# A two-part f16 GRU on one core: the candidate's matmul with both parts side by side, split into two matmuls onto one set of columns

## The reference

```python
def step(h, xs):
    xzt, xrt, xht = xs
    z = jax.nn.sigmoid(xzt + h @ U_z + vz)
    r = jax.nn.sigmoid(xrt + h @ U_r + vr)
    hh = jnp.tanh(xht + r * h @ U + vh)
    h_new = (1.0 - z) * h + z * hh
    return (h_new, h_new)
```

## Time and profile before

| | us |
|---|---|
| median of 2 runs | 6571.26 |
| the runs | 6569.87 and 6572.66 |
| the profiled execution | 6569.49 |
| its span, first to last instruction | 6567.7 |
| PE matmul / weight load busy | 5848.3 / 5500.4 |
| DVE / ACT busy | 5242.4 / 3454.6 |
| mean granted clock of PE | 0.997 |

### The profile page before, as it was taken

One profiled execution on the slowest core, in us unless ns is written; L12 is line 12 of the kernel. 1 busy time (PEld: TensorE's weight loads), 2 busy tenths in 40 slices (PEclk: granted clock), 3 DMA queues, 4 the chain that ended last, 5 costly groups with the idle time before them and its releaser, 6 DMA issues.

```text
span 6567.7 us, 486051 instructions
## 1 busy us (share of the span) xinstructions
PE 5848.3 (89%) x200312; PEld 5500.4 (84%) x200312; DVE 5242.4 (80%) x39096; ACT 3454.6 (53%) x23405; POOL 7.8 (0%) x22
## 2 busy tenths in 40 slices
PE   7888888888888888888888888888888888888888
PEld 7888888888888888888888888888888888888888
DVE  6888888878888888887888887888878888788887
ACT  3555555555555555555555555555555555555555
POOL 0000000000000000000000000000000000000000
PEclk8999999999999999999999999999999999999999
DMA  2000000000000000000000000000000000000000
GB/s 84 19 19 16 19 18 19 18 19 16 19 18 19 18 18 18 19 19 18 17 18 19 18 19 16 19 18 19 19 18 16 19 19 18 18 18 19 18 19 18
DMA packets 80316, 129.98 MB, mean 20 GB/s; under 512 B 12336, under 2 KB 18480, under 8 KB 80304
## 3 DMA queue, kind: packets, MB, share of 16 engines
q1 hardware_dynamic: 80304, 129.81, 5.7%
HBM read 20.46 MB, written 8.65 MB: 4 GB/s over the span
## 4 chain that ended last, share of the span: by engine, by line
DVE 50%; PE 31%; ACT 10%; issue 8%; DVEq 1%; POOL 0%; POOLq 0%
PE pair_r L299 31%; DVE rh_part L571 11%; DVE h_part L571 7%; DVE rh_part L578 7%; DVE pair_r L562 6%; DVE h_part L601 5%; DVE ps_z L562 5%; DVE pair_h L566 4%; ACT r_scan L434 4%; DVE h_part L609 3%; ACT pair_r L389 3%; ACT th_z L406 2%; DVEq L647 1%; PE ps_z L255 0%; DVE y_next L529 0%
## 5 line engine op out<-in xcount | busy, mean ns | idle before, releaser
L299 PEld LDWEIGHTS pair_r<-h_part,u_part 128*128 128x128 f16 x65568 | 1779.5, 96 | 1038.7 <-DVE h_part L571 1033.8
L299 PE MATMUL pair_r<-h_part,u_part 128*128 128x48 f16 (+1 forms) x65568 | 1976.9, 183 | 693.2 <-DVE h_part L571 686.5
L299 PE MATMUL pair_h<-rh_part,u_part 128*128 128x48 f16 (+1 forms) x65536 | 1953.4, 183 | 0.0
L299 PE MATMUL ps_z<-h_part,u_part 128*128 128x48 f16 (+1 forms) x65568 | 1942.9, 183 | 1.3 <-issue 1.3
L299 PEld LDWEIGHTS pair_h<-rh_part,u_part 128*128 128x128 f16 x65536 | 1797.6, 96 | 0.0
L299 PEld LDWEIGHTS ps_z<-h_part,u_part 128*128 128x128 f16 x65568 | 1784.7, 96 | 1.4 <-issue 1.4
L406 ACT ACTIVATE r_scan<-pair_r 128x4 f32<-128x4 f32 x4098 | 720.6, 176 | 1955.2 <-DVE pair_r L562 1752.6
L566 DVE TENSOR_REDUCE pair_h<-pair_h 128x4 f32<-128x8 f32 x4096 | 714.4, 175 | 549.9 <-PE pair_h L299 549.9
L562 DVE TENSOR_REDUCE pair_r<-pair_r 128x4 f32<-128x20 f32 x4098 | 766.5, 187 | 428.6 <-PE pair_r L299 2.7
L571 DVE TENSOR_TENSOR_SCAN rh_part<-r_scan,rh_part 128x12 f16<-128x12 f32 x4098 | 749.6, 183 | 140.5
L406 ACT ACTIVATE th_z<-ps_z 128x8 f32<-128x8 f32 x2048 | 362.7, 177 | 893.7 <-DVE ps_z L562 893.7
(11 more groups left out here) (75 smaller groups left out, 3111.3 us busy)
## 6 DMA issues: line engine op xcount, KB each, us to landing
w_stage<-w_in SPq DMA_DIRECT2D x384, 256.0 KB, 2.3
x_tok<-in_x SPq DMA_DIRECT2D x68, 128.0 KB, 2.6
out_dram<-o_tok SPq DMA_DIRECT2D x66, 128.0 KB, 2.3
mlp_w<-in_L_cond_W SPq DMA_DIRECT2D x2, 1024.0 KB, 6.8
u_raw<-in_L_cond_U_r SPq DMA_DIRECT2D x1, 1024.0 KB, 5.8
u_raw<-in_L_cond_U_z SPq DMA_DIRECT2D x1, 1024.0 KB, 7.8
u_raw<-in_L_cond_U SPq DMA_DIRECT2D x1, 1024.0 KB, 10.2
w_in<-in_L_cond_W_r SPq DMA_DIRECT2D x4, 256.0 KB, 9.6
```

Of the source, the lines that this page charges most:

```text
L299: return nc.tensor.matmul(to[:, :, :, 0:run], u_part[:, g, part, k, gm * P:(gm + 1) * P], runs.unsqueeze(1).broadcast_to([P, repeats, n, r ...
```

## The change

Each tile of H becomes two matmuls with the same weights, first the high parts, then the low parts, both onto the same PSUM columns, where they add up by themselves; each has 24 columns (the 12 of one part, streamed twice). With the sum already in the product's columns, DVE's two `candidate_total` and their semaphores go, and ACT's tanh reads the columns of the product directly, two by two at a stride, after PE's own signal. The zero slot of `xp` goes too, and with it the copy of zeros in H's seed. Because the tanh now reads the columns that H's next seed writes, ACT waits for the end of its second tanh before that seed.

```diff
-        xp = sb("xp", [P, GM, 2 * TB, 2, B])
+        xp = sb("xp", [P, GM, 2 * TB, B])
...
-            runs = banks.rearrange("p (m c) -> p m c", c=H_SLOT)[:, :, WIDE - PARTS * RUN:WIDE]
-            return runs.rearrange("p m (a c) -> p m a c", c=RUN)[:, :, :, STEP - 1:STEP * B:STEP]
+            return banks.rearrange("p (m c) -> p m c", c=H_SLOT)[:, :, STEP - 1:STEP * B:STEP]
...
-            nc.gpsimd.memset(xp[:, :, :, :, :], 0.0).then_inc(s["h0_ready"], 1)
+            nc.gpsimd.memset(xp[:, :, TB:2 * TB, :], 0.0).then_inc(s["h0_ready"], 1)
...
-                n = ADDENDS[g] if g == H else ADDENDS[g] - 1
+                n = PARTS if g == H else ADDENDS[g] - 1
                 at = k // HC * n * PITCH + k % HC * B * STEP
-
+                weights = u_part[:, g, part, k, gm * P:(gm + 1) * P]
+                runs = parts[:, at:at + n * PITCH].rearrange("p (a c) -> p a c", c=PITCH)
+
+                if g == H:
+
+                    repeats, run = (1, B * STEP) if closing else (WIDE // (n * RUN), RUN)
+                    to = bank[:, H_SLOT * m:H_SLOT * m + repeats * RUN].rearrange("p (r c) -> p r c", c=RUN)[:, :, 0:run]
+                    for a in range(n):
+                        last = nc.tensor.matmul(to, weights, runs[:, a, 0:run].unsqueeze(1).broadcast_to([P, repeats, run]),
+                                                start=False, stop=False, skip_group_check=True)
+                    return last
...
             def tanh(to, bank, g, n, wait, t1, done):
                 act.wait_ge(s[wait], t1)
-                at = H_SUM if g == H else SUM
-                A(to, bank[:, at:at + n], ACT.Tanh, scale=scale_reg[g]).then_inc(s[done], 1)
+                if g == H:
+                    A(to.rearrange("p (m b) -> p m b", b=B), candidate_cols(bank), ACT.Tanh, scale=scale_reg[g]).then_inc(s[done], 1)
+                else:
+                    A(to, bank[:, SUM:SUM + n], ACT.Tanh, scale=scale_reg[g]).then_inc(s[done], 1)
...
-                    tanh(n_scan[:, half[0], 1], ps_h[0], H, HS, "h0_sum", t1, "h0_th")
+                    tanh(n_scan[:, half[0], 1], ps_h[0], H, HS, "h0_mm", t1, "h0_th")
                     seed(ps_z, Z, nxt)
-                    tanh(n_scan[:, half[1], 1], ps_h[1], H, HS, "h1_sum", t1, "h1_th")
+                    tanh(n_scan[:, half[1], 1], ps_h[1], H, HS, "h1_mm", t1, "h1_th")
                     if proj is not None and u == K:
                         act.wait_ge(s["xp_ok"], act.snap(proj[2] + 1))
+
+                    act.wait_ge(s["h1_th"], t1)
                     seed(pair_h, H, nxt)
...
-            def candidate_total(hf):
-                V.tensor_reduce(ps_h[hf][:, H_SUM:H_SUM + HS].rearrange("p (m b) -> p m b", b=B),
-                                candidate_cols(ps_h[hf]).rearrange("p m a b -> p m b a"), AX_X, ALU.add).then_inc(s[f"h{hf}_sum"], 1)
...
-                dve.wait_ge(s["h0_mm"], t1)
-                candidate_total(0)
-
                 dve.wait_ge(s["z_keep"], t1)
...
-                dve.wait_ge(s["h1_mm"], t1)
-                candidate_total(1)
```

More of the change, by code:

```diff
@@ L110, in gru_kernel @@
         SUM = 256
-        H_SLOT, H_SUM = 256, 128
+        H_SLOT = 256
         def cols(bank, g, m0, m1):
@@ L127, in gru_kernel @@
                  "x_in x_tr y_ok y_copied proj0_mm proj0_ok wst_in proj_mm xp_ok o_sum o_tr o_ev out_st "
-                 "seed0 h_open h0_ready r0_mm r1_mm z_mm z_keep h_ok h0_mm h1_mm r0_sum r1_sum z_sum h0_sum h1_sum r0_th r1_th z_th h0_th h1_th "
+                 "seed0 h_open h0_ready r0_mm r1_mm z_mm z_keep h_ok h0_mm h1_mm r0_sum r1_sum z_sum r0_th r1_th z_th h0_th h1_th "
                  "rhi0 rhi1 rh0 rh1 khi keep_ok nhi0 nhi1 hs0 hs1 copied scan_zero rh_zero")
@@ L290, in tile @@
             def tile(bank, m, g, gm, k, part, parts, first=False, closing=False):
-                n = ADDENDS[g] if g == H else ADDENDS[g] - 1
+                n = PARTS if g == H else ADDENDS[g] - 1
                 at = k // HC * n * PITCH + k % HC * B * STEP
+                weights = u_part[:, g, part, k, gm * P:(gm + 1) * P]
[7 more added lines that the diff above has]
+                    return last
                 repeats, run = (1, B * STEP) if closing else (WIDE // (n * RUN), RUN)
-                runs = parts[:, at:at + n * PITCH].rearrange("p (a c) -> p a c", c=PITCH)[:, :, 0:run]
-                end = (H_SLOT if g == H else SLOT) * m + WIDE
+                end = SLOT * m + WIDE
                 to = bank[:, end - repeats * n * RUN:end].rearrange("p (r a c) -> p r a c", a=n, c=RUN)
-                return nc.tensor.matmul(to[:, :, :, 0:run], u_part[:, g, part, k, gm * P:(gm + 1) * P],
-                                        runs.unsqueeze(1).broadcast_to([P, repeats, n, run]),
-                                        start=first and g != H, stop=False, skip_group_check=True)
+                return nc.tensor.matmul(to[:, :, :, 0:run], weights,
+                                        runs[:, :, 0:run].unsqueeze(1).broadcast_to([P, repeats, n, run]),
+                                        start=first, stop=False, skip_group_check=True)
             def staggered(banks, g, parts, src, name, t1):
@@ L380, in seed @@
             def seed(banks, g, at):
+                src = xp[:, g * K:(g + 1) * K, at, :]
                 if g == H:
-                    return A(candidate_cols(banks.rearrange("p h c -> p (h c)")),
-                             xp[:, g * K:(g + 1) * K, at].rearrange("p m a b -> p m a b"), ACT.Copy)
-                src = xp[:, g * K:(g + 1) * K, at, 0]
+                    return A(candidate_cols(banks.rearrange("p h c -> p (h c)")), src, ACT.Copy)
                 if g == Z:
@@ L404, in tanh @@
                 act.wait_ge(s[wait], t1)
-                at = H_SUM if g == H else SUM
-                A(to, bank[:, at:at + n], ACT.Tanh, scale=scale_reg[g]).then_inc(s[done], 1)
+                if g == H:
+                    A(to.rearrange("p (m b) -> p m b", b=B), candidate_cols(bank), ACT.Tanh, scale=scale_reg[g]).then_inc(s[done], 1)
+                else:
+                    A(to, bank[:, SUM:SUM + n], ACT.Tanh, scale=scale_reg[g]).then_inc(s[done], 1)
             def store_projection(i, ring, bb):
-                return A(xp[:, i, bass.ds(ring, TB), 0, bb], ps_p[:, bb * TB:(bb + 1) * TB], ACT.Identity,
+                return A(xp[:, i, bass.ds(ring, TB), bb], ps_p[:, bb * TB:(bb + 1) * TB], ACT.Identity,
                          bias=v_bias[:, i, bb:bb + 1])
@@ L553, in _ @@
                 for bb in range(B):
-                    V.tensor_tensor(xp[:, g * K:(g + 1) * K, 0:TB, 0, bb], src[:, :, :, bb],
+                    V.tensor_tensor(xp[:, g * K:(g + 1) * K, 0:TB, bb], src[:, :, :, bb],
                                     v_bias[:, g * K:(g + 1) * K, bb:bb + 1].broadcast_to([P, K, TB]),
```

## The result

The changed kernel takes 7833.39 us (7829.21 and 7837.57), the kernel before 6571.26: the ratio is 1.1919, 95% interval 1.1891 to 1.1948. The profiled execution took 7829.21 us for a span of 7826.9. The forecast was 7705 in 7610 to 8100.

The account below looks back on a forecast made before the run. No engine alone bounds the kernel; a serial loop hands over between engines 2048 times. Steps of 3.72 us (3.14 + 0.58) give 7618.6, plus 82.6 around them 7701, and a slow first step makes 7705 us, range 7610 to 8100.

Parts of the forecast that it names:

- The spacing: PE's H product: each pair of weight load and 24-column matmul takes 25.0 ns, bounds 10 to 27.
- Half 1's chain: H's end, ACT's tanh, DVE's high part and scan, then R's second part: +0.58 us, step 3.14 to 3.72 us.
- The pause inside R: Sign on PE: R waits inside itself for half 1, about 0.2 to 0.3 us.
- The cover: Half 0's tanh, high part and R's first 13 matmuls, and the projection, hide behind half 1: no cost.
- The z chain: Z's tanh and factors on ACT, DVE's keep product: covered, ready at 3008.35, wanted at 3008.80.
- The sums' removal: DVE loses two candidate sums of 0.17 us each per step: gain 0.02 us a step, 40 us in all.
- rival A: PE's H spacing halves with the columns or dropped second loads; only the sums' removal remains: 6530 us. Chance 0.08.
- Rival C: PE is short of instructions, supply limited to the present mean rate: 4.2 us a step, 8730 us. Chance 0.04.
- B: PE's granted clock falls, 1.2 GHz throughout giving 4.47 us a step, 9240 us, or anything between. Chance 0.08.
- half 1's high part 3.61 us behind the start of R: Sign on DVE: if the high part starts at another distance, the sum is wrong in its second term.

Follow-up runs that it names:

- looped kernel: Changed kernel with PE's three plain steps of an outer turn as one step in a loop of 3, outputs transposed behind it: 7711.97 us, ratio 1.1741.

## Why the prediction was right, and where it was off

**The spacing** was taken as 25.0 ns, since 20 ns of columns already did not set it. (The rows, 184 - 173, give 11 ns for 24 columns and not 10, so 21 to 22 for 48, still less than 25.) Measured: 25.2 ns in the changed kernel's H stage, 24.9 by the kernel with 48 H matmuls. Every pair had its own load, as the identity's rows had suggested (265848 matmuls and 265848 loads). The Trainium skill (TensorE: Matmul & The Clock Gate, Back-to-back issue gap) was read too narrowly in the prediction: the section gives its formula for a matmul by itself, says that it counts too little for pairs of load and matmul at few columns, and its table puts 1 to 64 columns at a floor of about 25 ns. So it did not speak for the change, and the trace agrees with that floor at 24 columns as at 48.

**Half 1's chain.** From H's start the forecast had 1.78 us to the tanh and 1.99 to the high part; both were met to 0.01 us. The pause inside R was to be 0.2 to 0.3 us: it is 0.22 us between the starts of the 13th and 14th matmul behind a projection, and 0.34 without one (medians). The step was forecast at 3.72 and was 3.72 (looped kernel: 7711.97 us against 7701 of the sum). Step by step this part is right, and three kernels show it from three sides: fewer projections and a later half 0 change nothing, and 16 H matmuls less take their 25 ns each off.

**The cover.** Half 0 and PE's own issue cost nothing, as forecast (the kernels with half 0 closed later and with fewer projections). The z chain was not tried by itself, but DVE's product with its factor starts at 3016.60 in the changed kernel's trace, 0.45 us ahead of half 0's first use of DVE.

**The sums' removal** was the mis-sized term of rival A: 0.02 us a step in the text, 0.048 measured. It entered nothing but the rival's time, 6530 for 6476.63.

**The sum's missing term** is code: 116 us of the 128 by which 7833.39 exceeds 7705; of the rest, 7 us are what the looped kernel takes beyond the forecast, and 5 the difference between two measurements of the changed kernel. The range held the result, but its top had been set for a wider spacing and a clock that falls, not for this. That 116 us fit into it is luck. Rival C said that PE could be short of instructions, but as a supply rate, and it was dismissed because 25 ns held over 96 pairs. That says something on the rate and nothing on whether a loop's code stays. The number that would have decided it is the size of PE's outer body, 9 x 192 instructions growing to 9 x 256. The clock's fall is a follower of that pause: without the pauses the mean was 0.997. The text had said that a granted clock below 1 in the loop proves B. It was below 1 (0.62 in a window of 8 us) and did not prove B, which had the clock fall in steps without a pause. The narrower matmuls only made the time at the lower clock longer.

**A criterion that was badly put.** The text wanted half 1's high part 3.61 us behind the start of R. It is not: in the step shown it is 3017.70 - 3013.77 = 3.93, since R's start moves with the projection. From Z it is 3017.70 - 3014.91 = 2.79 us, for 2.21 before, and that is the +0.58.

## What to carry to other kernels

At the full clock a matmul of few columns costs its place in the stream and not its columns: two of 24 columns cost 50 ns where one of 48 cost 25. (At 1.2 GHz one of 48 took 39.7.) So splitting one to save a reduction pays only if that reduction stands on the path for longer than all the added matmuls. What the reduction is worth must be asked in both kernels: here it was worth 0.05 us a step before and 0.20 us after the split. And count the instructions of the longest loop body on each engine before adding to it: on PE the step over the limit cost more than 3 us in each turn, and folding plain steps into an inner loop took it back at no cost.

## What the runs showed that was not expected

- PE's outer body of 2048 matmul and load instructions and more is fetched again in each turn, with a pause of 1.6 us in the turn shown and 2.2 us at the longest, and a clock of 1.2 GHz for some us behind it; a body of 1792 and a few is fetched once. Together 3.7 us a turn on average. Why the pause differs from turn to turn, and why the lower clock ends sooner with 48 columns, stays open.
- A chain of waits that is 94% PE did not mean that PE was the bound: with three of four projections left out the time stayed within 0.1% (7709.92 for 7711.97). A pause that is shorter than about 0.2 us does not show in the rows of the matmuls, since each row lasts 0.18 us; it shows in their starts and in the rows of the weight loads.
